# Two layers of conditioned transformer on one core: layer 0's MLP weights loaded four and five slots later, their low parts made four slots later

## The reference, cut to what matters

```
mod = silu(c) @ w_mod + b_mod                      # six rows of 288 per sample
h   = layernorm(x) * (1 + scale) + shift
q, k, v = heads(h @ w_qkv + b_qkv)                 # 16 heads of 18
(layer 0 only: q, k = layernorm per head, times g_q, g_k)
o   = softmax(q k^T * 18**-0.5) v
x   = x + gate * (o @ w_proj + b_proj)
h   = layernorm(x) * (1 + scale2) + shift2
x   = x + gate2 * (gelu(h @ w1 + b1) @ w2 + b2)    # w1: 288 x 1152, w2: 1152 x 288
```

## Time and profile before

| quantity | value |
|---|---|
| median of 3 runs | 2560.09 us (2556.29 to 2560.41) |
| profiled execution, its own time | 2560.63 us |
| its span in the profile | 2558.8 us |
| PE busy | 2368.6 us (93%) |
| PE weight load busy | 1988.2 us (78%) |
| DVE busy | 1842.1 us (72%) |
| ACT busy | 1626.4 us (64%) |
| POOL busy | 708.4 us (28%) |
| mean DMA rate | 110 GB/s |

### The profile page before, as it was taken

The page is one execution under the profiler, slowest core; times in us unless marked ns, Lnnn a source line. Parts: engine busy times, 40 slices in busy tenths (PEclk is TensorE's granted clock), DMA queues, the critical chain, the costliest instruction groups (busy, mean ns, idle before and its releaser), DMA issues.

```text
span 2558.8 us, 56620 instructions
## 1 busy us (share of the span) xinstructions
PE 2368.6 (93%) x21219; PEld 1988.2 (78%) x21219; DVE 1842.1 (72%) x3456; ACT 1626.4 (64%) x3049; POOL 708.4 (28%) x938
## 2 busy tenths in 40 slices
PE   5568999999999999999899899999999999999998
PEld 3346878878888887887787788888888888888878
DVE  6357777777777777777677777777777777777764
ACT  3256666676676666666566666666676666666653
POOL 2012332332332333233222122222222222223212
PEclk8778999999999999999999999999999999999989
DMA  3776757757656666666856755565566655565531
GB/s 99 134 172 107 122 114 117 122 114 122 116 114 117 116 118 116 114 119 113 141 89 114 144 98 101 95 112 106 97 103 102 114 95 101 97 113 102 95 65 42
DMA packets 259208, 280.91 MB, mean 110 GB/s; under 512 B 25930, under 2 KB 243212, under 8 KB 258936
## 3 DMA queue, kind: packets, MB, share of 16 engines
q1 hardware_dynamic: 245840, 250.24, 56.4%
q10 hardware_dynamic: 13096, 27.04, 4.1%
HBM read 101.86 MB, written 26.73 MB: 50 GB/s over the span
## 4 chain that ended last, share of the span: by engine, by line
PE 50%; DVE 14%; DMA 12%; SPq 7%; issue 7%; POOL 5%; ACT 4%; DVEq 0%; POOLq 0%; ACTq 0%
PE psum L783 11%; DMA attn_k_stack<-attn_qk_hi 9%; PE psum L873 7%; SPq L1352 6%; PE psum_exp L783 5%; PE psum_max L783 5%; DVE attn_maxima L1093 5%; PE psum_exp L849 4%; PE psum L933 4%; PE psum L934 4%; PE psum L935 4%; PE psum_max L862 3%; DVE attn_qk_centred L1131 3%; POOL attn_qk_lo L1292 2%; PE psum L790 2%
## 5 line engine op out<-in xcount | busy, mean ns | idle before, releaser
L969 ACT ACTIVATE attn_probs<-psum_exp 128x1024 f32<-128x1024 f32 x512 | 527.0, 1029 | 401.1 <-PE psum_exp L849 388.2
L1093 DVE TENSOR_REDUCE attn_maxima<-psum_max 128x4 f32<-128x1024 f32 x512 | 620.4, 1212 | 90.1 <-PE psum_max L862 86.1
L1266 POOL TENSOR_TENSOR mlp_x<-mlp_x,mlp_gated 128x288 f32<-128x288 f32 x128 | 103.1, 805 | 1051.6 <-DVE mlp_gated L1110 1051.6
L783 PE MATMUL psum<-attn_ln_split,w_qkv_split 128*128 128x256 f32 (+3 forms) x2240 | 337.6, 296 | 10.1 <-DVE attn_ln_split L1200 6.8
L933 PE MATMUL psum<-mlp_w_fc_hi,mlp_hidden_hi 128*128 128x288 f32 x1152 | 341.7, 297 | 2.9 <-DVE mlp_w_fc_lo L770 2.0
L934 PE MATMUL psum<-mlp_w_fc_lo,mlp_hidden_hi 128*128 128x288 f32 x1152 | 341.4, 296 | 0.0
L935 PE MATMUL psum<-mlp_w_fc_hi,mlp_hidden_lo 128*128 128x288 f32 x1152 | 341.0, 296 | 0.0
L783 PEld LDWEIGHTS psum<-attn_ln_split,w_qkv_split 128*128 128x128 f32 (+3 forms) x2240 | 282.7, 182 | 59.1 <-issue 25.5
L862 PE MATMUL psum_max<-attn_k_stack,attn_q_stack 62*128 62x256 f32 x2048 | 218.9, 292 | 91.5 <-DMA attn_k_stack<-attn_qk_hi 62.7
L873 PE MATMUL psum<-attn_probs,attn_v 128*32 128x256 f32 x4096 | 282.7, 395 | 1.1 <-ACT attn_probs L969 1.1
L849 PE MATMUL psum_exp<-attn_q_stack,attn_k_stack 64*128 64x256 f32 x2048 | 260.2, 332 | 24.2 <-DMA attn_q_stack<-attn_neg_max_lo 12.0
(11 more groups left out here) (170 smaller groups left out, 4203.8 us busy)
## 6 DMA issues: line engine op xcount, KB each, us to landing
attn_q_stack<-attn_qk_hi SPq DMA_DIRECT2D x256, 128.0 KB
attn_k_stack<-attn_qk_hi SPq DMA_DIRECT2D x256, 128.0 KB
attn_o_and_sums<-attn_o_transposed SPq DMA_DIRECT2D x256, 128.0 KB, 5.0
mlp_gate_and_gated_bias<-modulation ACTq DMA_DIRECT2D x64, 288.0 KB, 4.1
attn_qk_squares<-qk_rstd SPq DMA_DIRECT2D x32, 512.0 KB
attn_q_stack<-attn_qk_lo SPq DMA_DIRECT2D x128, 128.0 KB
attn_k_stack<-attn_qk_lo SPq DMA_DIRECT2D x128, 128.0 KB
attn_x<-in_x_dram SPq DMA_DIRECT2D x32, 288.0 KB, 8.0
```

The source lines that it names most:

```text
L783: mm = q.matmul(to, lhs, rhs, start=(i == 0), stop=(i == 6))
L969: q.activation(probs[r][:], ps_exp[:], ACT.Exp, scale=SCORE_SCALE).then_inc(S["exps"], 1)
L1093: q.tensor_reduce(maxes[g % 2][:, p // QUARTER, :, p % QUARTER, :], ps_max[:].rearrange("p a (t n) -> p a t n", t=TT), AX.X, ALU.max).then ...
L1266: q.tensor_tensor(xt, xt, gated2[:], ALU.add).then_inc(S["added2"], 1)
```

## The change

Four numbers in two lines of constants change, all of layer 0 (the first entry of each pair). w1 is loaded in slot 24 instead of 20, w2 in slot 26 instead of 21. w1 is split in slots 36 (high) and 37 (low) instead of 32 and 33, w2 in 40 and 41 instead of 36 and 37.

```diff
-W_AT, W1_SPLIT, W2_SPLIT = (20, SPAN * (B - 1) + 51), (32, SPAN * (B - 1) + 58), (36, SPAN * (B - 1) + 64)
-W2_AT = (21, SPAN * (B - 1) + 59)
+W_AT, W1_SPLIT, W2_SPLIT = (24, SPAN * (B - 1) + 51), (36, SPAN * (B - 1) + 58), (40, SPAN * (B - 1) + 64)
+W2_AT = (26, SPAN * (B - 1) + 59)
```

## The result

The changed kernel takes 2561.4 us in the median of 20 runs, the kernel before on the same chip 2556.4 us in 20 runs: a ratio of 1.0018 (95% interval 1.0010 to 1.0026), 5.0 us slower. The forecast was 1.6 us faster. The time lies inside the range given, but the change has the other sign. Rival B is the nearest by the change, with +3.7, or +5.3 with the DVE term at its bound. That the time falls in the range is luck of the starting point: the forecast was counted from an execution of 2560.63 us, while 20 runs of the kernel before have their median 4.2 us lower. Counted as a change, the range goes from -6.6 to +3.9, and +5.0 lies outside.

What follows compares the result with a forecast made beforehand. PE bounds the kernel from the fifth slice on, carrying earlier shifts to the end: -5.6 (slot 20) - 0.2 (slots 20 to 36) + 4.2 (splits) = -1.6 against 2560.63, so 2559.0 us; range 2554 to 2564.5.

Steps and rivals of the forecast that it cites:

- Rival B: Slots 20 to 36: `mlp_x` comes behind w1 and w2, costing up to 5.1 us; total +3.7, 2564.3 us; chance 0.17.
- the DVE term: Slots 37 to 43: later splits add DVE work ahead of PE's L941; +4.2 us, bounds 2.7 to 5.8.
- `mlp_x` beside the loads: Slots 20 to 36: `mlp_x` pays half of w1's 6.3 us and lands at +15.2; stretch gains 0.2 us.
- the bound and the half: Slots 20 to 36: all of w1 and half of w2 pass `mlp_x` (5.1 us loss), or half of w1 (0.2 gain).
- The term for slot 20: Stack DMAs to slot 20: freed of w1's load, PE starts 5.6 us earlier; bounds 4 to 6.7.
- Rival C: Slot 20 is not relieved, w1 only filled gaps; gain there 0 to 1.5 us; total +3.2, 2563.8 us; chance 0.06.
- The term for the splits: Slots 37 to 43: DVE's extra 4.3 us of splitting delays L941 and slot 52; +4.2 us.
- Rival D: Slots 37 to 43: DVE work hides, only 1.5 of 4.3 us arrive; total -4.3, 2556.3 us; chance 0.12.
- The way out: The per-head norm factor's way out at slot 22, freed of w2's load: near 4 us instead of 7.4.
- the factor's return: The per-head norm factor's way back, slots 20 to 36: expected at +11.5 after the factor's issue, before at +14.2.
- The placed maxima: Small placement of maxima for slot 32, in SP's queue: some 4 us later, but hidden in PE's idle time.

Runs made afterwards that it cites:

- e1: Against the kernel before: only the loads moved, w1 to slot 24 and w2 to slot 26, splits left at 32 and 36; ratio 1.0005.
- e3: Against the kernel before: only w1's load moved, from slot 20 to 24; w2's load and both splits as before; ratio 1.0006.
- e4: Against the kernel before: only w2's load moved, from slot 21 to 26; w1's load and both splits as before; ratio 1.0005.
- e11: Against the kernel before: w2 loaded in slot 13 and w1 in slot 24, splits as before; ratio 1.0004.
- e12: Like e1, but w1's first DMA cut into four of 288 columns, in both layers; ratio to the kernel before 1.0016.
- e2: Against the kernel before: only the splits moved four slots later, to 36 and 40, loads as before; ratio 1.0020.
- e10: Against the kernel before: only w2's split moved, from slot 36 to 46; loads and w1's split as before; ratio 1.0006.
- e5: Against the kernel before: layer 0's two loads issued by SP in slot 26, right behind `mlp_x`, splits as before; ratio 1.0003.
- e13: Against the kernel before: layer 0's w1 load issued by SP in slot 26, w2's by SP in slot 29, splits as before; ratio 0.9988.
- e8: Against the kernel before: w2 loaded in slot 13, behind a wait its slot there needs, everything else as before; ratio 1.0017.

## Why the prediction was wrong, point by point

**The step that failed** is `mlp_x` beside the loads: "issued at +5.3, that is +12.0, plus half of w1's 6.3 us, about 3.2: +15.2. I take a gain of 0.2 us in slots 20 to 36." It was issued at +5.3 and came at +20.1, and the stretch lost 5.0 us; with the loads alone (e1) 5.5, with w1's alone (e3) 5.3. This is rival B, at its price of 5.1 us. The mis-sized term is what the loads cost `mlp_x`: 3.2 us stated, 8.1 measured (14.86 us from its issue, against 6.75 before), and 9.5 in e1. Two readings had been at hand for how much passes ahead, the bound and the half, and I took the half without a row that showed it. The one row there was, the way out beside w2, had lost 3.8 us to a load of 4.3; taken as "nearly all" and not as "not everything", it gives 12.0 + 6.3 and a part of w2's 4.3 us, and that is what came. e4 (4.1 of 4.3), e11 (6.1 of 6.3) and e3 (8.2 of 10.6) show the same three times more.

**What the two queues did.** Neither reading describes it. Packets, MB and share of 16 engines of ACT's queue (q10) and SP's (q1) in e1, from 167 to 170 us and from 170 to 182.5, where `mlp_x` lands; then w2's row, whose last number is the time from its issue (165.46) to its landing:

```profile
q10 hardware_dynamic: 157, 0.71, 83.1%
q1 hardware_dynamic: 82, 0.17, 20.3%
...
q1 hardware_dynamic: 955, 1.57, 53.8%
q10 hardware_dynamic: 950, 1.46, 53.2%
...
mlp_w_fc_raw<-in_L_cond_w_dram ACTq DMA_DIRECT2D x1, 1296.0 KB, 22.5
```

In the last 12.5 us the queues move packet for packet, 955 to 950. The Trainium skill (DMA: Bandwidth & Descriptors, queues, rings and completion order) has each DMA engine take turns between queues packet by packet, and in this part the trace agrees. Nor were the loads served whole in order of issue: w2 lands at 188.0, 5.4 us after `mlp_x`.

Two things made the turns cost more than half of w1. First, ACT's queue has the lead at the start: 157 packets to 82, of some 4.5 KB each against 2. In e3 SP's queue moves no packet from the issue of the way out (164.62) to 168.9 us, and ACT's 905; in the kernel before none in the 2.5 us from 168.0 on, and ACT's 294. So the 7.4 us of the way out, which the prediction took as agreeing with turns, did not show them. Why ACT's queue gets this lead no run shows; e12's smaller rows did not take it away. Second, I set `mlp_x` against w1 alone. Between its issue and its landing (166.42 to 182.5) SP's queue moved 1,054 packets, the factor's way back ahead of `mlp_x` among them, and ACT's queue 1,134, which are 2.30 MB of the loads' 2.96. How the loss divides between the two is not shown.

So rival B came out in its place and its price: the small transfers lost from 71% (e12, 7.5 of 10.6 us) to 97% (e11) of the loads' packet time. Service in order of issue, which the prediction tied to that bound, is not what happened. The same section of the Trainium skill says that a DMA's semaphore increment lands only after every earlier write of that DMA engine, in whatever queue. This would hold back `mlp_x` too, but no run here isolates it.

**The term for slot 20,** -5.6, was right. The profile after alone has -4.5; the eight values of slots 4 to 20 with w1 gone from there and w2 not in slot 13 average 45.2 us, the five with w1 there 50.6: -5.4. Rival C is out.

**The term for the splits,** +4.2, was right in size and in its working. L941 comes 4.3 us later after slot 36's L862, in the profile after and in e2; the stretch is 5.1 and 3.8 us longer. L941's idle time, 4.19 and 2.87 us, falls short of the 4.6 stated, since part of the delay shows at PE's instructions before it. e10 adds that the 2.8 us of slot 37 had themselves cost only 0.9; the 4.3 us on top of them count in full. Rival D is out.

**The way out** at 4.0 us was right, **the factor's return** at +17.9 wrong (+11.5), for the same reason as `mlp_x`, with DVE's idle time before it doubled (7.20 us, before 3.58). It is not the last to arrive: DVE's second `attn_gated` waits for POOL, 1.10 us more. **The placed maxima** came 2.9 us later (L849 at 190.11) and cost nothing (L849 idle for 2.8 us, slot 36 still waiting for its stacks), as stated.

**The sum anew:** -5.4 at slot 20; slots 20 to 36, mean of after, e1 and e12 (48.7) less that of before, e2 and e10 (43.0), +5.7; slots 36 to 52, mean of after and e2 (45.3) less that of before and e1 (40.7), +4.6. Together +4.9, measured +5.0 (2.6 to 6.6 by the interval). By timing alone: loads +0.05% (not told from nothing), splits +0.20%, both +0.18%. What was expected to pay for the DVE work, slot 20, is given back one sample later, and the DVE work stays as the loss.

**Why moving the loads gains nothing** I take to be the sum of the traffic: wherever the loads stood, from slot 13 to 37, something that PE waits for stood beside them and came later. This is argued from the single runs; no run leaves the loads out. By the stretches e5 (4.9 us) and e13 (3.3) find room, by timing neither is shown to.

**Open:** e5's profiled execution is 4.1 us shorter than before's, and its first three stretches 4.9, yet ten timed runs show nothing (1.0003); nor do the runs tell why one execution differs from another by some 3 us at the change of layers, nor where e8 and e12 lose the 3 us that their stretches do not show.

## What to carry to other kernels

Whoever moves a weight load away from one latency-bound chain must be ready to pay most of its packet time again, here 71 to 97%, on the small transfer that is issued beside it in another queue, or (in e3) 1.45 us ahead of it. Look for a stretch in which PE, and not a DMA, is last, before moving it. To price such a transfer, look at the packets of everything in its queue up to it, and not only at its own bytes (argued from the counts above, not tested by itself). A load that may be late is best put behind the urgent transfer in that transfer's own queue, with everything urgent that follows in that queue checked too. And once an engine's row has no idle time left ahead of what PE waits for, every microsecond added to it counts in full; a first piece may still hide in the gaps.

## What the runs showed of the hardware

A small DMA in one queue lost most of the packet time of a large one in the other, also of one issued shortly after it (11.84 us instead of 3.6 for 128 KB in e3, w1 issued 1.45 us later; with w2 alone beside it 7.4, before). With work in both queues their packets went one for one (955 to 950 in 12.5 us, e1), after a start in which ACT's queue had the lead. Cutting the large DMA's rows from 4,608 to 1,152 bytes changed the delay by no more than 2 us. Within one queue the order of issue protects the earlier one: `mlp_x` ahead of the 2.96 MB of loads in SP's queue took 5.75 us from its issue, beside the same loads in ACT's queue 14.9 (after) and 16.2 (e1).
